# A two-layer attention and sign-product graph kernel: VectorE's second score read moved ahead of a split, and the last layer's first result row finished one step later

## What is computed

```python
def _gat_layer(x, W, adj):                      # used twice
    Wh, Ws = jnp.split(x @ W, 2, axis=-1)
    a = jax.nn.softmax(Wh @ Ws.T, axis=-1) * adj
    return jax.nn.leaky_relu(a @ Wh + x, 0.01)

x = _layernorm(x + gat(gat(x)), axis=-1)
signs = jnp.maximum(jnp.sign(x), 0.0) @ jnp.sign(weight).T
x = _layernorm(x + jax.nn.relu(adj @ signs), axis=-1)
```

## Time and profile before

| | |
|---|---|
| median of 3 runs | 2357.22 us (2354.26 to 2358.11) |
| the profiled execution's own time | 2370.51 us |
| its span, first to last instruction | 2368.7 us |
| TensorE matmul busy, of the span | 2140.0 us (90%) |
| VectorE busy | 1521.9 us (64%) |
| ScalarE busy | 918.4 us (39%) |
| GpSimd busy | 703.4 us (30%) |
| mean granted TensorE clock | 0.969 |

### The profile page before, as it was taken

One profiled execution on the slowest core, in us unless ns is written; L12 is line 12 of the kernel. 1 busy time (PEld: TensorE's weight loads), 2 busy tenths in 40 slices (PEclk: granted clock), 3 DMA queues, 4 the chain that ended last, 5 costly groups with the idle time before them and its releaser, 6 DMA issues. The chain is left out here.

```text
span 2368.7 us, 38787 instructions
## 1 busy us (share of the span) xinstructions
PE 2140.0 (90%) x13260; PEld 1299.1 (55%) x13260; DVE 1521.9 (64%) x3933; ACT 918.4 (39%) x2071; POOL 703.4 (30%) x677
## 2 busy tenths in 40 slices
PE   3995999999999999994895999999999999997699
PEld 1443666666666666652333666666666666664244
DVE  3664677777777777774564566666666766666254
ACT  5663433443343343333563433433333343332000
POOL 1772222222232232222673222222222222221000
PEclk9997999999999999997997999999999999999799
DMA  5887667777777766754888677787767768765775
GB/s 173 167 176 158 135 145 153 154 148 154 157 149 148 154 148 138 156 118 140 194 185 181 145 151 156 154 170 154 158 151 158 163 147 169 155 140 130 244 242 185
DMA packets 735312, 378.99 MB, mean 160 GB/s; under 512 B 642064, under 2 KB 655376, under 8 KB 733456
## 3 DMA queue, kind: packets, MB, share of 16 engines
q1 hardware_dynamic: 724304, 340.77, 63.0%
q0 software_dynamic: 3328, 22.16, 6.7%
q10 hardware_dynamic: 7488, 13.63, 1.8%
HBM read 204.60 MB, written 59.64 MB: 112 GB/s over the span
## 5 line engine op out<-in xcount | busy, mean ns | idle before, releaser
L790 PE MATMUL p_out_a<-values,probs_t_a 128*128 128x512 f16 x4056 | 961.2, 380 | 0.4 <-DVE acc_a L997 0.4
L766 PE MATMUL p_scores_a<-keys_t,q_t_a 128*128 128x256 f16 x6552 | 819.3, 276 | 101.2 <-DVE peaks_a L933 53.5
L920 POOL TENSOR_TENSOR row_a<-row_a,adj_rows_a 128x512 f32<-128x512 f32 (+1 forms) x364 | 438.1, 1220 | 1286.2 <-ACT row_a L876 1279.5
L766 PEld LDWEIGHTS p_scores_a<-keys_t,q_t_a 128*128 128x128 f16 x6552 | 642.0, 99 | 302.5 <-DVE peaks_a L933 68.5
L790 PEld LDWEIGHTS p_out_a<-values,probs_t_a 128*128 128x128 f16 x4056 | 398.0, 98 | 374.9 <-issue 4.2
L868 ACT ACTIVATE row_a<-p_scores_a 128x256 f32<-128x256 f32 x468 | 178.8, 382 | 819.4 <-PE p_scores_a L766 818.3
L978 DVE SCALAR_TENSOR_TENSOR halves_a<-row_a,halves_a 128x512 f16<-128x512 f32 (+1 forms) x364 | 263.1, 723 | 196.8 <-ACT halves_a L889 195.5
L500 PE MATMUL p_rows_p<-w_p,x_t_p 128*128 128x512 f16 x1248 | 280.9, 386 | 86.8 <-DMA x_t_p<-x_p 86.5
L997 DVE SCALAR_TENSOR_TENSOR acc_a<-acc_a,factor_a,p_out_a 128x512 f32<-128x512 f32 x312 | 233.1, 747 | 166.2 <-PE p_out_a L790 161.2
L876 ACT ACTIVATE row_a<-row_a,shift_a,scales 128x512 f32<-128x512 f32 (+1 forms) x364 | 280.6, 772 | 93.1 <-DVE shift_a L968 93.1
L933 DVE CUSTOM_DVE_ANT_0 row_a<-row_a,p_scores_a 128x256 f32<-128x256 f32 x468 | 196.3, 420 | 115.5 <-PE p_scores_a L766 110.2
(11 more groups left out here) (101 smaller groups left out, 1319.6 us busy)
## 6 DMA issues: line engine op xcount, KB each, us to landing
adj_rows_a<-adj_rows SPq DMA_DIRECT2D x312, 256.0 KB, 3.3
adj_t<-adj_blocks POOLq DMA_DIRECT2D x104, 208.0 KB, 3.9
adj_b<-adj_t SPq DMA_DIRECT2D x26, 832.0 KB, 4.5
s_rows<-sum_rows_p SPq DMA_DIRECT2D x26, 512.0 KB, 2.9
x_rows_a<-x_rows SPq DMA_DIRECT2D x52, 256.0 KB, 3.6
values<-x_rows SPq DMA_DIRECT2D x13, 512.0 KB, 5.4
adj_rows_a<-adj_rows SPq DMA_DIRECT2D x52, 128.0 KB, 2.7
x_mid<-work_a SPq DMA_DIRECT2D x26, 256.0 KB, 3.3
```

The lines of the kernel that those rows point to most:

```text
L766: last = pe.matmul(bank(w, name), queries(pair_of(w), q_block, qh, c), keys_t[:, kh, k_block, c, cols], start=(first and c == 0 and n == 0 ...
L790: last = pe.matmul(p_out[:, u], probs_t[:, turned_slot(w), u, ph * tiles + j, :], values[:, 4 * step_of(w) + j, vh, :], start=(j == 0 and ...
L920: pool.tensor_tensor(piece, piece, adj_rows[:, n % ADJ_RING, 0:width(w)], ALU.mult).then_inc(masked, 1)
```

## The change

VectorE's `read_second(w)` moves from behind `split(w-1, 1)` to ahead of it, in both layers. In the last layer, `make_y` of the first tile, the store of its row and the transpose of its bits move from step 4 to step 5; its sign product, the copy and the store of that from step 6 to step 7, which is step 0 of the pair after. The second tile's stay. The semaphore `products_stored` becomes one per slot, and `add_rows` and the end of the stage wait for the slot's own count.

```diff
@@ sp
-                        for t, at in late_tiles(w, 4, 6):
+                        for t, at in late_tiles(w, 5, 6):
                             store(t)
                             turn_bits(t)
-                        for t, at in late_tiles(w, 6, 8):
+                        for t, at in late_tiles(w, 7, 8):
                             store_products(t)
...
-                    sp.wait_ge(products_stored, 16 * T)
+                    for u in (0, 1):
+                        sp.wait_ge(products_stored[u], 16 * J)
@@ pe
-                    made_now = list(late_tiles(w, 6, 8)) if last_layer else []
+                    made_now = list(late_tiles(w, 7, 8)) if last_layer else []
@@ act
-                    for t, at in late_tiles(w, 6, 8) if last_layer else ():
+                    for t, at in late_tiles(w, 7, 8) if last_layer else ():
                         keep_product(t)
@@ dve, add_rows
-                                dve.wait_ge(products_stored, 16 * (2 * i - 1 + u))
+                                dve.wait_ge(products_stored[u], 16 * i)
@@ dve
-                    for t, u in late_tiles(w, 4, 6) if last_layer else late_tiles(w, 3, 4):
+                    for t, u in late_tiles(w, 5, 6) if last_layer else late_tiles(w, 3, 4):
                         make_y(t // 2, u)
                     if 0 <= w - 1 < windows:
                         split(w - 1, 0)
                     if 0 <= w - LAG < windows:
                         add_total(w - LAG)
                         accumulate(w - LAG, 0)
+                    if w < windows and wide(w):
+                        read_second(w)
                     if 0 <= w - 1 < windows:
                         split(w - 1, 1)
-                    if w < windows and wide(w):
-                        read_second(w)
                     if 0 <= w - LAG < windows:
                         accumulate(w - LAG, 1)
```

More of the change, by code:

```diff
@@ L134, in build @@
             "adj_checked", "pad_zeroed", "weight_loaded", "negative_made", "signs_made", "signs_turned",
-            "above", "bits_turned", "sign_products", "products_kept", "products_stored")}
+            "above", "bits_turned", "sign_products", "products_kept")}
         sems.update({name: [sem(f"{name}{r}") for r in range(count)] for name, count in (
-            ("x_loaded", 4), ("x_turned", 4), ("keys_turned", 2), ("adj_loaded", 3), ("row_loaded", 2), ("first_loaded", 2), ("stored", 2),
+            ("x_loaded", 4), ("x_turned", 4), ("keys_turned", 2), ("adj_loaded", 3), ("row_loaded", 2), ("first_loaded", 2), ("stored", 2), ("products_stored", 2),
             ("project_chain", LAYERS), ("attend_chain", LAYERS), ("adj_cast", LAYERS))})
@@ L715, in store_products @@
                     sp.wait_ge(products_kept, t + 1)
-                    sp.dma_start(products_out[t * P:(t + 1) * P, :], product_rows[:, t % 2]).then_inc(products_stored, 16)
+                    sp.dma_start(products_out[t * P:(t + 1) * P, :], product_rows[:, t % 2]).then_inc(products_stored[t % 2], 16)
                 turn_queries(0)
```

## The result

The changed kernel takes 2335.2 us (median of four runs, 2334.61 to 2338.03) against 2357.46 (2354.26 to 2358.11): a ratio of 0.9903, 95% interval 0.9886 to 0.9919, 22.3 us less. On another chip it was 2334.67 against 2362.39, ratio 0.9879 (0.9858 to 0.9901), 27.7 us less. The forecast was 2316, faster by 41. The sign and the wide range (2302 to 2340) held, but the size was nearly twice what came, and 2335 lies outside the 2306 to 2328 that the prediction gave its own case: it is the number of its rival 1.

A forecast was written before the change was run, and what follows sets the result against it. TensorE sets the pace of both attention stages; only its idle time and clock can be won. 11.2 + 7.3 + 31.6 - 15.6 + 6.8 = 41.3 us off the median 2357.22 gives 2316, within 2306 to 2328; wide range 2302 to 2340.

The forecast's parts named there:

- rival 1: Earlier read brings nothing because ScalarE's copy comes late, or step 5 stalls instead; 23 us gained, 2334; chance 0.12.
- Part 1, layer 0: Steps 2 and 3 of layer 0: the earlier read gains 0.93 us per pair, 11.2 us in all.
- Part 1, last layer: Step 2 of the last layer: the earlier read gains 12 x 0.61 = 7.3 us, which step 3 keeps.
- Part 2, step 4: Last layer: moving the first tile's make_y to step 5 removes the load wait and step-4 stalls, 31.6 us.
- 1.4 to spare: Step 5, last layer: VectorE has 4.8 us of room against 3.4 of moved work; a mask collision adds 1.1.
- Part 3, the new wait: Step 0, last layer: the moved sign product waits for the accumulate, 1.3 us taken per pair, 15.6 us lost.
- the term for the bits: Step 6: L1040 waits for the first tile's turned bits, 0 to 0.3 us, up to 3.3 with longest landing.
- the signs: Wrong if: stall at step 5 or 6, idle before L1040, gap over 3 us before L809, half clock behind gaps.
- The clock: Last layer: four clock drops behind step-4 stalls, 1.7 us each, expected to go; 6.8 us gained.
- rival 2: Each new stall brings half clock, 20 us, and the 6.8 don't come; 14 us gained, 2343; chance 0.08.
- Rival 3: Slower: late bits in step 6 hold L1040, then splits, accumulates and TensorE's sign product; 2366; chance 0.06.
- rival 4: Nothing gained: the stalls exist mainly under the profiler, whose execution is 13 us longer; 2357; chance 0.05.

The follow-up runs named there:

- e10: e6 with layer 0's two result rows made at steps 4 and 5 instead of 3 and 4; 2306.53 us, ratio 0.9774 to the kernel before.
- e1: The kernel before with the earlier read alone, make_y and sign product staying at steps 4 and 6; 2352.06 us against 2362.28, ratio 0.9959.
- e4: The changed kernel, unchanged, run on another chip beside the kernel before; 2334.67 us, ratio 0.9879.
- e3: The changed kernel with the sign product of step 0 put behind the first two score products; 2319.46 us, ratio 0.9815 to the kernel before.
- e6: The changed kernel with the edits of both e3 and e8; 2314.12 us, ratio 0.9791 to the kernel before.
- e8: The changed kernel with the first tile's store and transpose of bits issued earlier in step 5, behind the first transpose of halves; 2327.47 us, ratio 0.9860.
- e2: The changed kernel with read_second back behind the split, so the later first row alone; 2350.77 us, ratio 0.9943 to the kernel before.
- e0: The kernel before, unchanged, profiled a second time on another chip; profiled execution 2363.6 us, median of 17 runs 2362.28.
- e9: The kernel before with the earlier read and load_first issued in step 3 ahead of the first transpose of halves, make_y at step 4; 2316.01 us, ratio 0.9815.

## Why the prediction was right, and where its size was off

**What bounds it**: right. In eleven kernels the pairs became shorter or longer by TensorE's waits and the clock behind them, while its work stayed the same.

**Part 1, layer 0**: right in mechanism, 11.2 us forecast; 65.52 to 64.72 is 0.80 a pair, 9.6 us. Seven of the eleven pairs gained 0.87 to 0.89, two 0.65, one 1.17, and one only 0.15, in which step 3 has a stall of 1.20 us after the change. That VectorE's unbroken run would let only part of the stall go was confirmed: step 3 kept 0.6 us in most pairs, which e10 removed.

**Part 1, last layer**: 7.3 us at step 2 over the twelve pairs, as forecast; but e1 shows that it belongs to both parts together. Taken alone, a pair kept 0.26 of it. The prediction added it as if it stood by itself.

**Part 2, step 4**: right; 31.6 us forecast, 31.3 measured over the twelve pairs between the two profiles, and no stall at step 5 in this profile. The 31.6 held a small misreading: of the 25 waits of the earlier trace rows twelve, not thirteen, are step 2's, and one of 1.30 us lies in the first pair, so that the stalls of step 4 were 29.1 us and not 29.8.

The collision with GpSimd's mask came in every pair, but at another operation than the one the prediction looked at. From the timeline of step 5 of one pair after the change:

```profile
1366.15 0.69 DVE L1028 SCALAR_TENSOR_TENSOR work_a<-work_a 128x512 f32<-128x512 f32 x1
1366.36 3.27 POOL L921 TENSOR_TENSOR row_a<-row_a,adj_rows_a 128x512 f32<-128x512 f32 x2 [5.73 <-ACT row_a L877]
1366.88 1.64 DVE L1031 TENSOR_TENSOR work_a<-work_a,x_rows_a 128x512 f32<-128x512 f32 x1
```

L1031 of the first tile took 1.64 us in twelve of thirteen pairs, where all 26 of L1030 had taken 0.69 before, and L1037 kept its 0.49. These 0.95 us are less than the 1.4 to spare, so TensorE lost nothing by them. In e4 one pair has a stall of 0.55 us at step 5, and this is what stands in its timeline:

```profile
1430.89 2.94 POOL L921 TENSOR_TENSOR row_a<-row_a,adj_rows_a 128x512 f32<-128x512 f32 x2 [5.73 <-ACT row_a L877]
...
1431.04 1.67 DVE L1028 SCALAR_TENSOR_TENSOR work_a<-work_a 128x512 f32<-128x512 f32 x1
...
1432.74 1.64 DVE L1031 TENSOR_TENSOR work_a<-work_a,x_rows_a 128x512 f32<-128x512 f32 x1
...
1438.55 0.83 PE L767 MATMUL p_scores_a<-keys_t,q_t_a 128*128 128x256 f16 x6 [0.55 <-DVE peaks_a L934]
```

Here L1028 too started behind GpSimd's mask and took 1.67 us instead of 0.69. Together the two lost 1.9 us, more than the 1.4 to spare. The same pair has this stall in every other profile of a kernel with the later row (0.56 us in e3, e6, e8 and e10, 1.15 in e2, where the read stands behind the split); the one profile without it is that of the result. So the prediction's room of 1.4 us and its price of a collision, 1.1, were about right, and costing it at nothing holds for one collision a pair, not for two.

**Part 3, the new wait**: the mechanism, its place, its twelve occurrences and its lower size were right (1.1 us forecast with the hidden tail, 0.89 + 0.15 measured). The step that failed is the term for the bits. I let the transpose go out "at 1532.1, or up to 0.8 later if SP is still at the one before", and took 0 to 0.3 us of wait for L1040 from the medians. Relative to the start of step 6 that is 1.4 to 2.2 us; in the pair shown above it went out 4.0 us in, because a transpose of halves held SP for 3.14 us. That is no rarity: 49 of the last layer's 182 transposes of halves took over 2 us, and 43 in the profile of before, which the median of 1.24 hides. VectorE waited 10.0 us there in five pairs. In all the new wait cost 17.2 + 12 x 0.15 = 19.0 us, against 15.6. With the half clock behind it, two of the signs that the prediction had named for being wrong came true in some pairs, and six of the twelve gaps were under its 1.0 us.

**The clock**: I expected all four drops to go; two remained, 3.4 us. They follow the wait of 2.80 us and one of the two of 2.3, none of those up to 1.76. So rival 2 was right for some of the long waits and wrong for the short ones: of the Trainium skill's frequent short idles that bring the clock down (TensorE: Matmul & The Clock Gate, "A second HAM failure mode") nothing shows at 0.89 us a pair, here or in e8.

**The sum**: with these sizes, 9.6 + 7.3 + 31.3 - 19.0 + 3.4 = 32.6 us, 8.7 less than the 41.3 forecast; 3.4 of that is the bits, 3.4 the clock, 1.6 layer 0 and 0.3 part 2. The two profiled executions differ by 2370.5 - 2334.6 = 35.9; the other 3.3 are the first pair of layer 0, 65.06 us before and 61.73 after. Against its own like, 2329.2, the forecast was thus 5.4 us low. The other 14 of the 19 us come from the step "I take the difference from the median": the profile of before lay 13.3 us above its median, that of after 0.6 below its own. Terms read from an execution with more stalls than most were subtracted from the time of the others. e0 says that about half of its 7 us over the second profile was such stalls; that the rest of the gap to the median was made of the same, I argue and have not shown.

**The rivals**: none of them came as written. The measured time is the number of rival 1, 2334, by luck: its reason, a copy too late for the earlier read, did not come, for layer 0 and step 2 gained what that read was to bring. Rival 3's mechanism, L1040 held by late bits, is what happened, with 17.2 - 12 x 0.89 = 6.5 us beyond what the accumulate alone costs, where 57 would have been needed in all. Of rival 4, stalls that are larger under the profiler, e0 shows that single executions differ in them; the gain itself refutes the rest of it.

## What to carry to other kernels

When a stall ends with a wait for a transfer, look at where in its queue that transfer is issued before moving the work that waits: issuing the load ahead of the step's transposes instead of behind them (e9) beat a step's delay of five operations on four engines by 15 us. A piece of work that is moved meets the waits of its new place, so list every semaphore that it waits for and what is ahead of it there, and what runs beside each of its operations; a few matmuls ahead of it can hide such a wait (e3). And gains of several edits against one stall are not terms of a sum: measure each alone and both together, and take sizes from more than one execution, against that execution's own time.

## What the runs showed of the hardware that was not expected

SP's issue of a transpose of the same size took 1.24 us in the median, but over 2 us in 49 of 182 and up to 3.6 (3.14 in the row above), and everything behind it in the queue moved.

VectorE's operations with two inputs in SBUF took 0.69 us when they started ahead of GpSimd's mask, even where it began while they ran, and about 1.65 when the mask had started first: L1031 of the changed kernel 0.69 in twelve cases of the one kind and 1.64 in twelve of the other, L1028 1.67 in the one case in e4. L1033, the statistics of one input of the same size, took its 0.69 beside the mask 24 times. This agrees with the exclusive port pair of SBUF — State Buffer, "SBUF: two separate sides", in the Trainium skill, which goes to whichever starts first for its whole instruction; the prediction had looked for it only at L1036.
